# A graph network's scatter pass: seven of twelve tiles by DMA with addition, one-hots by ScalarE, and two fill tiles in the kept passes

## The reference

```python
h = relu(layernorm(x)); x = x + clip(h + segsum(h[src] * w_e, dst) + .1 * h)          # weighted
h = relu(layernorm(x))                                                                 # the scatter pass
m = silu(einsum('ei,ej,ijh->eh', h[dst], edge_attr_8, W_msg_tp) / sqrt(128)) @ W_msg_lin / 4
agg = segment_sum(m, src, num_segments=12500)       # gathers by dst, sums by src
x = x + h + update(h, agg)
h = relu(layernorm(x)); x = x + relational(h, edge_attr_16, edge_type_90)              # relational
h = relu(layernorm(x)); w = kernel_net(edge_attr_6).reshape(-1, 16, 16)
for i in range(4):                                  # depth 0 computes w, depths 1 to 3 read it back
    msg = einsum('ei,eio->eo', h[src], w)
    h = gelu(segment_sum(msg, dst) * inv_deg + h @ root_W[i] + root_b[i])
```

## Time and profile before

| | |
|---|---|
| runs | 27549.18, 27579.13, 27592.92 us; median 27579.13 |
| the profiled execution's own time | 27545.35 us |
| its span in the profile | 27543.6 us |
| PE busy | 22500.5 us, 82% |
| POOL busy | 22669.1 us, 82% |
| DVE busy | 17653.1 us, 64% |
| ACT busy | 14700.1 us, 53% |
| mean granted clock of TensorE | 0.88 of full |

### The profile page before, as it was taken

How to read it: one execution, slowest core, us unless ns; L and a number is a source line. 1 busy time by engine, 2 the same in 40 slices (tenths; PEclk the granted TensorE clock), 3 DMA queues, 4 the chain that set the end, 5 groups by cost and what they waited for, 6 DMA issues and landing times. The chain is left out here.

```text
span 27543.6 us, 413278 instructions
## 1 busy us (share of the span) xinstructions
PE 22500.5 (82%) x110422; PEld 12380.9 (45%) x110422; DVE 17653.1 (64%) x29340; ACT 14700.1 (53%) x24676; POOL 22669.1 (82%) x30933
## 2 busy tenths in 40 slices
PE   7888848888879999968888886888868888688886
PEld 3444435555556666634444443333333333343333
DVE  5555548888878888844444444666656666566665
ACT  6666601111117777733333333777757777577775
POOL 7888868888868888878888888888878888788887
PEclk9999979999989999977777777999989889799888
DMA  3111135555542222222322323555545555455554
GB/s 89 34 34 34 39 59 94 92 94 93 93 83 74 75 75 76 75 76 96 97 96 96 97 95 92 163 163 163 163 129 165 163 163 163 129 168 162 163 162 127
DMA packets 2192590, 2964.46 MB, mean 108 GB/s; under 512 B 778166, under 2 KB 1678244, under 8 KB 2190948
## 3 DMA queue, kind: packets, MB, share of 16 engines
q1 hardware_dynamic: 1340898, 2776.49, 30.8%
q0 software_dynamic: 782304, 157.92, 8.7%
q10 hardware_dynamic: 69282, 28.92, 0.4%
HBM read 2289.02 MB, written 672.64 MB: 108 GB/s over the span
## 5 line engine op out<-in xcount | busy, mean ns | idle before, releaser
L772 POOL DMA_INDIRECT got<-table,idx x14040 | 13761.8, 980 | 3764.0 <-issue 3473.8
L790 PE MATMUL in_place<-place_hot,tparts 128*128 128x512 fp8e4 x49950 | 12164.8, 405 | 2750.4 <-ACT place_hot L995 2462.5
L995 ACT ACTIVATE place_hot<-place_b,far_lanes 128x512 fp8e4<-128x512 f16 x17550 | 10959.8, 704 | 12.3 <-PE in_place L790 11.3
L790 PEld LDWEIGHTS in_place<-place_hot,tparts 128*128 128x128 bf16 x49950 | 5076.0, 103 | 9118.6 <-issue 4170.7
L775 POOL MEMSET rest<- 128x256 f32 x14040 | 4686.2, 334 | 8.3
L1599 POOL DMA_INDIRECT added<-rows,add_idx x2160 | 3599.9, 1667 | 719.3 <-issue 655.2
L1171 DVE TENSOR_TENSOR prod<-w_in,rows_p 128x2048 f32<-128x2048 f32 x810 | 1853.1, 2288 | 2837.4 <-issue 1522.9
L1216 DVE TENSOR_TENSOR prod<-wcopy,got 128x1024 f32<-128x1024 f32 x810 | 968.6, 1223 | 2603.3 <-DMA got<-table,idx 2324.8
L1642 PE MATMUL acc<-hot,spread 128*128 128x392 bf16 x12960 | 2533.4, 349 | 0.0
L859 PE MATMUL wmat<-k,h 128*128 128x256 f32 x6480 | 2045.2, 446 | 0.0
L1225 DVE TENSOR_REDUCE msg<-prod 128x64 f32<-128x1024 f32 x1620 | 1969.0, 1215 | 41.4
(11 more groups left out here) (250 smaller groups left out, 23056.3 us busy)
## 6 DMA issues: line engine op xcount, KB each, us to landing
w_in<-kept SPq DMA_DIRECT2D x2430, 512.0 KB
kept<-wcopy SPq DMA_DIRECT2D x810, 512.0 KB
got<-table,idx POOLq DMA_INDIRECT x14040
attr<-in_edge_attr SPq DMA_DIRECT2D x270, 768.0 KB
place_b<-place_row SPq DMA_DIRECT2D x1350, 128.0 KB
range_b<-range_row SPq DMA_DIRECT2D x1350, 128.0 KB
rows<-in_src_row SPq DMA_DIRECT2D x270, 512.0 KB
sums<-outb SPq DMA_DIRECT2D x1350, 96.0 KB
```

Source lines behind the costliest of these rows:

```text
L772: pool.indirect_dma_start(out=got[:, r, j * W:(j + 1) * W], out_offset=None, in_=table, in_offset=bass.IndirectOffsetOnAxis(ap=idx[:, r, j ...
L790: mm = pe.matmul(in_place[b][:, h, :], tparts[:, s, t, :], place_hot[:, b, t, h * XC:(h + 1) * XC], start=(t == 0 and s == 0), stop=(t == ...
L995: ins = act.activation(place_hot[:, b, t, :], place_b[:, b, :], ACT.Abs_reciprocal_sqrt, bias=SB["far_lanes"][:, t:t + 1], scale=HOT_SLOPE ...
```

## The change

In the scatter pass seven tiles of a chunk go by DMA and five by TensorE. The one-hots of the places are made by ACT instead of DVE, with the function that the other passes use, in fp8 instead of bf16: DVE only works out the five biases of a chunk (`lanes_of`). ACT makes the one-hots of chunk k-1 in its turn k, two before `silu(k)` and three behind `take_starts(k+2)`. The sums come out of PSUM times 2^-5 and are scaled back once. Two of the added tables, loaded into the place of a one-hot buffer before, get a tile of their own. In the kept passes the memsets of a chunk go to one of two `rest` tiles by turn, and POOL waits for `rested` of one chunk earlier. ACT's prologue now peels `HALVES * 2` turns.

```diff
-ADDED = 8
+ADDED = 7
 HOT = C - ADDED
@@ edge_pass
-        rest = sb("rest", [P, J0 * RW])
+        FILLS = HALVES if kind == "kernel_kept" else 1
+        rest = sb("rest", [P, FILLS, J0 * RW])
...
-                    if at != 0:
-                        pool.wait_ge(S["rested"], k)
+                    if at is None or at >= FILLS:
+                        pool.wait_ge(S["rested"], k - FILLS + 1)
                     pool.sem_inc(S["turn_open"], 1)
...
-                        ins = pool.memset(rest[:, j * RW:(j + 1) * RW], 0.0)
+                        ins = pool.memset(rest[:, r % FILLS, j * RW:(j + 1) * RW], 0.0)
@@ edge_pass_scatter
-        hot = sb("hot", [P, HALVES, HOT, RANGE], BF16)
+        hot = sb("hot", [P, HALVES, HOT, RANGE], F8)
+        hot_bias = sb("hot_bias", [P, HALVES, HOT])
+        tables = sb("tables", [P, 2 * NQ * D])
@@ ACT
+                    def places(k, b, tiles, at):
+                        if 0 in tiles:
+                            act.wait_ge(S["bias_made"], k + 1)
+                            if at is None or at >= HALVES:
+                                act.wait_ge(S["scattered"], k - 1)
+                            act.sem_inc(S["act_open"], 1)
+                        for j in tiles:
+                            act.activation(hot[:, b, j, :], SB["iota_place"][:, :], ACT.Abs_reciprocal_sqrt,
+                                           bias=hot_bias[:, b, j:j + 1], scale=HOT_SLOPE, saturate=False).then_inc(S["hot_made"], 1)
...
                             repeat(k + 1, 1 - b, None if at is None else at + 1)
+                        if behind:
+                            places(k - 1, 1 - b, range(0, 2), late)
                         silu(k, b, at)
                         if at is None or at + 2 < CHUNKS:
                             take_starts(k + 2, b, i + 1, None if at is None else at + 2)
+                        if behind:
+                            places(k - 1, 1 - b, range(2, HOT), late)
@@ DVE
-                    def places(k, b, tiles):
-                        for j in tiles:
-                            dve.tensor_scalar(hot[:, b, j, :], SB["iota_place"][:, :], SB["splace"][:, bass.ds(k * C + j, 1)],
-                                              None, ALU.is_equal).then_inc(S["hot_made"], 1)
+                    def lanes_of(k, b, at):
+                        if at is None or at >= HALVES:
+                            dve.wait_ge(S["hot_made"], (k - 1) * HOT)
+                        dve.tensor_scalar(hot_bias[:, b, :], SB["splace"][:, bass.ds(k * C, HOT)], -HOT_SLOPE, PLACE_SHIFT * HOT_SLOPE,
+                                          ALU.mult, ALU.add).then_inc(S["bias_made"], 1)
...
                         product(k, b, i, 1, at)
+                        lanes_of(k, b, at)
                         if behind:
                             spread_out(k - 1, 1 - b, c, late)
-                            places(k - 1, 1 - b, range(0, 2))
                         if at is None or at >= 2:
                             take_rows(k - 2, b)
                         product(k, b, i, 2, at)
-                        if behind:
-                            places(k - 1, 1 - b, range(2, HOT))
...
-                        dve.tensor_copy(result[:, k * RCOLS:(k + 1) * RCOLS], acc[k][:, 0:RCOLS]).then_inc(S["taken_out"], 1)
+                        dve.tensor_scalar(result[:, k * RCOLS:(k + 1) * RCOLS], acc[k][:, 0:RCOLS], 1.0 / HOT_IS, None, ALU.mult).then_inc(S["taken_out"], 1)
```

More of the change, by code:

```diff
@@ L701, in load @@
                         store(k - HALVES, b)
-                    if kind == "weighted" and at is not None and at >= CHUNKS - ADDED // 2:
+                    if kind == "weighted" and at is not None and at >= CHUNKS - -(-ADDED // 2):
                         clear_added(2 * (CHUNKS - 1 - at), 2 * (CHUNKS - at))
                 def clear_added(y0, y1):
-                    for y in range(y0, y1):
+                    for y in range(y0, min(y1, ADDED)):
                         sp.dma_start(SB["added"][y][0:NP_, :].rearrange("(p n t) f -> p n (t f)", p=P, t=FILL),
@@ L1513, in edge_pass_scatter @@
         turned = hot[:, 0, :, :].rearrange("p j c -> p (j c)").bitcast(F32)[:, 0:KT * P].rearrange("p (n c) -> p n c", n=KT)
-        spare = hot[:, 1, :, :].rearrange("p j c -> p (j c)").bitcast(F32)
-        tables_in = [SB["rows"][:, 0:NQ * D], spare[:, 0:NQ * D], spare[:, NQ * D:2 * NQ * D], SB["rows"][:, NQ * D:2 * NQ * D]]
+        tables_in = [SB["rows"][:, 0:NQ * D], tables[:, 0:NQ * D], tables[:, NQ * D:2 * NQ * D], SB["rows"][:, NQ * D:2 * NQ * D]]
         agg = SB["agg"][:, 0:NQ * D]
@@ L1519, in edge_pass_scatter @@
                  "msg_made", "silu_made", "cut", "spread_made", "hot_made", "scattered", "same_made", "same_summed", "rows_made",
-                 "dve_step", "turn_open", "lower_made", "taken_out", "turned_p", "turned_s", "out_stored", "out_back",
+                 "dve_step", "bias_made", "hot_open", "act_open", "turn_open", "lower_made", "taken_out", "turned_p", "turned_s", "out_stored", "out_back",
                  "table_in0", "table_in1", "table_in2", "table_in3", "table_taken"] + [f"added{y}" for y in range(ADDED)]
@@ L1639, in scatter @@
                         pe.wait_ge(S["hot_made"], k * HOT + j + 1)
+                        pe.sem_inc(S["hot_open"], 1)
                         for s in range(SPLITS):
@@ L1716, in turn @@
                             repeat(k + 1, 1 - b, None if at is None else at + 1)
+                        behind = at is None or at >= 1
+                        late = None if at is None else at - 1
+                        if behind:
+                            places(k - 1, 1 - b, range(0, 2), late)
                         silu(k, b, at)
@@ L1723, in _ @@
                     repeat(0, 0, 0)
-                    chunks(act, turn, HALVES, HALVES)
+                    chunks(act, turn, HALVES * 2, HALVES)
+                    places(CHUNKS - 1, 1, range(HOT), CHUNKS - 1)
                 @block.vector
@@ L1854, in _ @@
                     spread_out(k, 1, c, k)
-                    places(k, 1, range(HOT))
                     first_of_same(k, 1, k // HALVES, c, k)
```

## The result

| | before | after |
|---|---|---|
| median of the runs, us | 27586.03 (4 runs) | 27967.11 (4 runs, 27959.85 to 27985.15) |
| ratio, 95% interval | | 1.014 [1.0124, 1.0155] |
| span of the profiled execution | 27543.6 | 27959.6 |
| granted clock, mean | 0.880 | 0.874 |
| first to last gather or add of a pass, us: scatter | 4262 | 4568 |

The forecast was 27392 us with a range of 27030 to 27750; the measured time lies above it. The scatter pass lost 306 us (forecast +300). The kept passes should have given back 484 us. Their loops, from first to last gather, lost 17.8 + 19.1 + 27.3 = 64, and with the work behind each loop they lost more: from the first gather of the first kept pass to the end of the program it is 27543.6 - 17119.9 = 10423.7 us before and 27959.6 - 17439.0 = 10520.6 us after, 97 us longer.

A forecast was written before the change was run, and what follows sets the result against it. POOL was taken as the bound in the scatter pass and, by its supply of gathers, in the kept passes. -484 (kept) + 300 (scatter) - 3 (ends) = -187 us gave 27392 us beside the median, range 27030 to 27750.

The forecast's parts named there:

- Scatter pass: Scatter pass: a chunk goes from 15.79 to 16.9 us (bounds 16.0 and 18.0), +300 us in all.
- The cost of a switch: Scatter pass, ACT: each change between Silu and the one-hots' function costs one table load, 1.30 us, twice a chunk.
- Rival B: Scatter pass: a switch costs about twice the load, ring 18.2 us, total 27737 us, slower; chance 0.09.
- Rival A: Scatter pass: the ring does not bind, PE sets the pace at 15.6 or about 14.4 us; 26720 to 27040 us; chance 0.12.
- the ring: Scatter pass: `same`, `st` load, `take_starts`, table load, three one-hots, `lanes_of`, back to `same`; 16.9 us, sets the pace.
- The gap at a chunk's start: Kept passes, POOL: the gap before a chunk's first gather falls from 0.77 to 0.17 us with two fill tiles.
- The prediction's own sign: Kept passes: the prediction is wrong if the chunk stays above 12 us.
- the next limit: Kept passes: at 11.8 us a chunk ACT and those behind it have time to spare, so the gain is kept.
- The term of -484: Kept passes: 0.60 us saved at each of 3 x 269 chunk starts, -484 us (at least 379).
- Rival C: Kept passes: fill tiles bring nothing, the 0.60 us being the cost of waits and loop; 27876 us; chance 0.07.

The follow-up runs named there:

- scatter_alone: The changed kernel with one fill tile (`FILLS = 1`), so the scatter pass's half of the change alone: 1.0109 of the kernel before, +301 us.
- bias_late: scatter_alone with DVE's `lanes_of` moved behind `same` and the indices, last in its turn: 0.9827 of the kernel before, 477 us faster.
- no_silu: scatter_alone with Copy for Silu on the scatter pass's messages, so ACT keeps one table (outputs not the reference's): 0.997 of the kernel before, -82 us.
- fills_292: fills_alone with fills of 292 columns instead of 256 in the kept passes: 0.9847 of the kernel before.
- late_292: bias_late with two fill tiles and fills of 292 columns in the kept passes: 0.9807 of the kernel before.
- spare_table: The changed kernel with an eighth table in DRAM declared but never used, restoring the addresses of the kernel before: 1.0039 of the kernel before.
- fills_alone: The kernel before with only the two fill tiles of the kept passes: 0.9927 of the kernel before, 200 us faster.
- fewer_sums: fills_alone with 25 of PE's 37 matmuls in place in the kept passes, the third piece of the rows left out: 0.996 of the kernel before.
- wider_fills: fills_alone with fills of 328 columns instead of 256 in the kept passes: 0.9915 of the kernel before, 235 us faster.

## Why the prediction was wrong, step by step

*Scatter pass: right, to the term.* Medians over the 235 turns from 4000 to 8000 us, forecast in brackets: `same` to `take_starts` 4.69 (4.7), starts and mask 0.80 (0.80), table load with its seams 1.31 (1.30), three one-hots 4.59 (4.6), release 0.14 and `lanes_of` to `owner` 0.13 (together 0.35), `owner` to the end of `same` 5.09 (5.15). Sum 16.75; the mean turn is 16.98, since in 60 turns `lanes_of` starts more than 0.5 us behind the last one-hot: it waits for DVE's product and not for ACT. So that 16.9 was met to 0.1 us is in part luck. scatter_alone's +301 against the forecast +300 settles the size, bias_late and no_silu the mechanism.

*The cost of a switch.* In the turn shown the load starts 0.02 us behind the mask and the one-hots 0.01 us behind the load, with ACT busy before it; ahead of all 236 loads of this kind ACT idles 4.2 us. Rival B's doubled switch does not occur. The Trainium skill (ScalarE: Activation LUTs, What ACT_TABLE_LOAD costs) has a drain of some 1380 ns beside the load of 1283 ns. The trace agrees on the load, 1283 ns each time, and has no drain: from the end of the mask to the first one-hot it is 1.31 us.

*Rival A* asked what PE does if the ring doesn't bind. bias_late answers: 14.04 us a chunk at a granted clock of 1.00, below the 14.4 taken there. The ring did bind in the changed kernel, so rival A did not come true there.

*The gap at a chunk's start: right, and worth nothing by itself.* It went from 0.77 to 0.17 us, as forecast. POOL's own chunk became 8 x 1.445 = 11.56 us, even less than the 11.8 of the sum. The prediction's own sign came true beside it: the chunk stayed above 12 us.

*The step that failed* is the sentence behind it: "What could eat it is the next limit at 12.37 - 0.60 = 11.8 us a chunk. ACT waits for data in nearly every one of its 784 chunks there, so it and those behind it have time to spare." The wait showed slack at 12.37 us; it didn't say how much, nor what the others do once POOL no longer holds them. The runs show that they keep step wherever POOL's chunk is 11.87 us or more, in one kernel of two at 11.8 (fills_292: 419 us gained, near the 484; late_292 stalls), and in none below. At POOL's 11.56 us the chunk of the changed kernel is 12.39 us. The term of -484 came out as +64 us in the loops and +97 us with their ends. after_wider slows the fills of the changed kernel and changes nothing else: its loops are 3246 to 3247 us where the changed kernel's are 3340 to 3348. Rival C had nearly this number (27876), for a reason that is false: the 0.60 us were not the cost of waits and of the loop, as they went.

*What stays open.* That PE's signals come late and its matmuls in slow steps is shown. So is that this goes with POOL's own chunk, its gathers, fills and pause together: with the pause a cadence of 1.44 us is in step, and without it one of 1.48 us is. PE's work, POOL's lead and the lack of pauses do not decide it by themselves. What passes between POOL and PE, and what decides at 11.8 us, is not shown, nor is why two programs with the same kept passes, spare_table and the changed kernel, differ by 100 us a pass. The cadence was moved by the fills alone (their width, or none); whether fewer gathers of more rows do the same wasn't tried.

## What to carry to other kernels

A wait that one engine ends in every turn shows that the others have slack, not how much; before taking time off that engine, try it with its work made a little shorter and a little longer, for the whole can be fastest with a slightly slower producer. When work moves to an engine, look for what is queued behind its slowest input: a wait for it, put ahead of the instruction that starts that input, closes a ring, and one line moved to the turn's end opens it. Two halves of a change are best timed apart: here one cost 301 us, the other gave 200 alone, and together they lost 381.

## What the runs showed of the hardware

- **PE's steps beside POOL's.** In the third kept pass of fills_alone 563 matmuls start 0.5 to 1.5 us behind the one before them, 480 us in all; in the kernel before 33 do, 39 us in all. Of the 555 of them that follow a gather's start by less than 1.6 us, 361 start 0.2 to 0.4 us behind it and 172 start 0.9 to 1.1 us behind it, when POOL's fill begins; 22 lie elsewhere. In the changed kernel it is 213 and 39 of 523, and in fewer_sums 21 and 9 of 339, so not every stalled kernel has its steps at POOL's starts. In the rows of the changed kernel above, the matmuls at 25002.98, 25004.44 and 25005.93 stand 0.35, 0.36 and 0.41 us behind the gathers at 25002.63, 25004.08 and 25005.52.
- **Late signals.** In the kept passes of fills_alone `in_place_made` rises on average 0.5 to 1.0 us behind the end of the last sum within 18 us of POOL's last pause of over 0.5 us, and 7.2 to 7.9 us behind it after more than 30 (where no rise is recorded within 11 us, the record is taken as lost). In fewer_sums it is 0.9 to 1.5 us, 7.5 to 8.5 us between 18 and 30, and 1.6 to 1.8 us after more than 30, and wider_fills, with no pause at all, has 1.3 us: the time since the last pause doesn't explain the delay.
- **The clock.** In the scatter pass PE's granted clock was 0.93 with PE busy 86%, 0.92 with 91%, 0.97 with 94% and 1.00 without a gap (the kernel before, the changed one, no_silu and bias_late). In the last three PE has the same matmuls, and it is busy 15.5, 14.6 and 14.0 us a chunk: what takes PE's last pauses away gives more than the pauses.
- A cadence of 1.249 us a gather instead of 1.441, with the fills left out, made the kept passes some 120 us longer each (no_fills).
